# A recurrent block on one core: output product in three passes, a norm moved to ScalarE, a subtraction to GpSimd

## The reference, cut to what matters

```python
x = layernorm(x, ln0_w, ln0_b)
for l in range(4):
    h = layernorm(x, ln1_w[l], ln1_b[l]); hh = time_shift(h)
    xk, xv, xr = (h * m + hh * (1 - m) for m in (tmk[l], tmv[l], tmr[l]))
    k, v, sr = xk @ Wk[l].T, xv @ Wv[l].T, sigmoid(xr @ Wr[l].T)
    x = x + (sr * wkv(time_decay[l], time_first[l], k, v)) @ Wo[l].T
    h = layernorm(x, ln2_w[l], ln2_b[l]); hh = time_shift(h)
    xk, xr = (h * m + hh * (1 - m) for m in (cmk[l], cmr[l]))
    kf = square(relu(xk @ Wck[l].T))          # 256 -> 1024
    kv = kf @ Wcv[l].T                        # 1024 -> 256
    x = x + sigmoid(xr @ Wcr[l].T) * kv
```

## Time and profile before

| | us |
|---|---|
| median of 3 runs | 1927.9 |
| range of the runs | 1927.41 to 1932.6 |
| the profiled execution, its own time | 1932.82 |
| its span in the trace | 1931.1 |
| end of the recurrent part's last output product | about 741 |

### The profile page before, as it was taken

One profiled execution on the slowest core, in us unless ns is written; L12 is line 12 of the kernel. 1 busy time (PEld: TensorE's weight loads), 2 busy tenths in 40 slices (PEclk: granted clock), 3 DMA queues, 4 the chain that ended last, 5 costly groups with the idle time before them and its releaser, 6 DMA issues. The chain is left out here.

```text
span 1931.1 us, 26354 instructions
## 1 busy us (share of the span) xinstructions
PE 1812.3 (94%) x10124; PEld 1536.1 (80%) x10124; DVE 1233.3 (64%) x1953; ACT 841.0 (44%) x1304; POOL 2.7 (0%) x24
## 2 busy tenths in 40 slices
PE   2499999999999997999899999999999999999997
PEld 1277887777887776777689998899998899998996
DVE  6889999899998844677554454454454454454445
ACT  2565776666766543333233333333333333333333
POOL 0000000000000000000000000000000000000000
PEclk9699999999999998999789999999999999999999
DMA  3000000001001003111020000000000000001001
GB/s 109 6 22 17 12 27 34 6 28 39 1 12 49 1 1 95 42 42 36 11 76 33 34 25 10 33 33 33 33 18 14 33 33 33 33 11 60 1 1 39
DMA packets 35274, 56.54 MB, mean 29 GB/s; under 512 B 3094, under 2 KB 20476, under 8 KB 34684
## 3 DMA queue, kind: packets, MB, share of 16 engines
q1 hardware_dynamic: 35196, 55.47, 8.8%
HBM read 51.79 MB, written 3.67 MB: 29 GB/s over the span
## 5 line engine op out<-in xcount | busy, mean ns | idle before, releaser
L1489 DVE TENSOR_TENSOR hf<-sil,fbanks 128x512 f32<-128x512 f32 (+1 forms) x128 | 79.4, 620 | 332.2 <-PE fbanks L1658 273.4
L1597 ACT ACTIVATE sil<-fbanks 128x512 f32<-128x512 f32 (+1 forms) x128 | 69.6, 544 | 442.2 <-PE fbanks L1658 442.2
L1674 PE MATMUL fbank<-wl,hh 128*128 128x256 f32 x896 | 250.3, 279 | 0.0
L1674 PE MATMUL fbank<-wh,hl 128*128 128x256 f32 x896 | 250.1, 279 | 0.0
L1674 PE MATMUL fbank<-wh,hh 128*128 128x256 f32 x896 | 250.1, 279 | 0.0
L715 PE MATMUL pair<-wcv,kf 128*112 128x256 f32 x768 | 176.2, 379 | 0.0
L1489 DVE TENSOR_TENSOR hf<-sil,fbank 128x512 f32<-128x512 f32 (+1 forms) x128 | 79.5, 621 | 149.7 <-PE fbank L1658 142.7
L1674 PEld LDWEIGHTS fbank<-wl,hh 128*128 128x128 f32 x896 | 168.3, 188 | 2.2
L1674 PEld LDWEIGHTS fbank<-wh,hh 128*128 128x128 f32 x896 | 168.4, 188 | 1.8
L1674 PEld LDWEIGHTS fbank<-wh,hl 128*128 128x128 f32 x896 | 168.4, 188 | 0.0
L1496 DVE TENSOR_TENSOR hl<-hf,hh 128x512 fp32r<-128x512 f32 (+1 forms) x256 | 158.2, 618 | 0.0
(11 more groups left out here) (235 smaller groups left out, 3495.1 us busy)
## 6 DMA issues: line engine op xcount, KB each, us to landing
raw<-in_w_gate SPq DMA_DIRECT2D x16, 512.0 KB, 3.8
raw<-in_w_up SPq DMA_DIRECT2D x16, 512.0 KB, 4.7
raw<-in_w_down SPq DMA_DIRECT2D x16, 512.0 KB, 5.6
raw<-in_w_ck SPq DMA_DIRECT2D x4, 1024.0 KB, 4.8
wcv<-in_w_cv SPq DMA_DIRECT2D x4, 768.0 KB, 4.4
raw<-in_ctx_t SPq DMA_DIRECT2D x4, 750.0 KB, 6.3
ct<-in_ctx_t SPq DMA_DIRECT2D x4, 750.0 KB, 5.1
x<-in_x SPq DMA_DIRECT2D x4, 448.0 KB, 6.1
```

The source lines that it names most:

```text
L1489: dve.tensor_tensor(hf[i][:, 0:w], sil[i][:, 0:w], bank[2 * i + 1][:, 0:w], ALU.mult).then_inc(hf_ready, 1)
L1597: act.activation(sil[f % 2][:, 0:w], bank[2 * (f % 2)][:, 0:w], ACT.Silu).then_inc(sil_ready, 1)
L1674: ins = pe.matmul(bank[4 + 2 * (t % 2) + i // 2][:, (i % 2) * C:(i % 2 + 1) * C], a[t % 2][:, f, i * P:(i + 1) * P], m[h][:, DOWN + f * C: ...
```

## The change

The output product with `Wcv` takes three float32r passes for all eight blocks, and its loop runs over pairs of blocks on the outside and sequences inside: pairs 0 and 1 before `turn(1)`, pairs 2 and 3 behind it. It waits for each pair's `kfl`. The whole of `wcv` is staged and split (`wcvh`, `wcvl` of 2048 columns), and the float32 `wcv` and its DMA go. ScalarE rounds all four pairs to `kfh`. GpSimd subtracts to make `kfl`, in place of `kf`, and VectorE's `low_kf` goes. `ckl` takes the place of `mix_ck` in the same manner, and `diff` shares `dk`, for which `wkv_out` gets two waits. The second norm's `xn2` is made by ScalarE with a `shift` of its own, behind `norm_out(1)`, and the first norm's `normalise` moves ahead of `rsqrt0(2)`. On VectorE `wkv_numerator` moves ahead of `difference(1)`.

```diff
-        wcvh, wcvl = sb("wcvh", [P, SPLIT * C], F32R), sb("wcvl", [P, SPLIT * C], F32R)
-        wcv = sb("wcv", [P, (F // P - SPLIT) * C])
+        wcvh, wcvl = sb("wcvh", [P, FT * C], F32R), sb("wcvl", [P, FT * C], F32R)
...
-        shift = sb("shift", [T, G])
+        shift = {k: sb(f"shift{k}", [T, G]) for k in (1, 2)}
...
-        diff = sb("diff", [P, CB, G, T])
-        mixed = {n: sb("mix_" + n, [P, CB, G, T]) for n in ("k", "v", "r", "ck", "cr")}
+        mixed = {n: sb("mix_" + n, [P, CB, G, T]) for n in ("k", "v", "r", "cr")}
...
+        diff = dk
...
-        ckh, ckl = sb("ckh", [P, CB, G * T], F32R), sb("ckl", [P, CB, G * T], F32R)
-        kf = [sb(f"kf{i}", [P, 2, G * T]) for i in range(4)]
-        kfh, kfl = sb("kfh", [P, SPLIT, G * T], F32R), sb("kfl", [P, SPLIT, G * T], F32R)
+        ckh = sb("ckh", [P, CB, G * T], F32R)
+        with nc.sbuf_tensor("mix_ck", [P, CB, G, T], FP32) as t:
+            mixed["ck"] = t
+        ckl = sb("ckl", [P, CB, G * T], F32R)
+        with nc.sbuf_tensor("kf", [P, FT, G * T], FP32) as t:
+            kf = [t[:, 2 * j:2 * j + 2] for j in range(FT // 2)]
+        t = sb("kfl", [P, FT, G * T], F32R)
+        kfl = [t[:, 2 * j:2 * j + 2] for j in range(FT // 2)]
+        kfh = sb("kfh", [P, FT, G * T], F32R)
...
+            for m in range(STEPS):
+                for j in range(FT // 2):
+
+                    pool.wait_ge(kfh_ready, FT // 2 * m + j + 1)
+                    pool.tensor_tensor(kfl[j], kf[j], kfh[:, 2 * j:2 * j + 2], ALU.subtract).then_inc(kfl_ready, 1)
...
-                    ("cr", wcr, cr_done, 1), ("cv", wcv, cv_done, 2))
+                    ("cr", wcr, cr_done, 1))
...
-                if name == "cv":
-                    w = w[:, 0:SPLIT * C]
...
-                    t = tile if n == "cv" else tile[:].rearrange("p b c -> p (b c)")
-                    sp.dma_start(t[:, :], w[:, -t.shape[1]:]).then_inc(w_in[n], 16)
+                    sp.dma_start(tile[:].rearrange("p b c -> p (b c)"), w).then_inc(w_in[n], 16)
...
-            def set_shift(m):
-
-                dve.scalar_tensor_tensor(shift[:], mean[1], -1.0, rstd[1][:], ALU.mult, ALU.mult)\
-                    .then_inc(shift_ready, 1)
+            def set_shift(k):
+
+                dve.scalar_tensor_tensor(shift[k][:], mean[k], -1.0, rstd[k][:], ALU.mult, ALU.mult)\
+                    .then_inc(shift_ready[k], 1)
...
             def wkv_out(m):
 
                 dve.wait_ge(rec_ready, m + 1)
+                dve.wait_ge(mix1_ready, 6 * min(m + 2, STEPS))
+                if m:
+                    dve.wait_ge(mix2_ready, 4 * m)
                 after(did(dve.tensor_tensor(tokens(dk), tokens(dp), at(e1b, 1), ALU.mult)))
                 n = did(dve.scalar_tensor_tensor(tokens(dk), tokens(dk), 2.0, at(e1b, 1), ALU.subtract, ALU.mult))
                 dve.wait_ge(num_ready, m + 1)
...
-            def low_kf(m, j):
-
-                dve.wait_ge(kfh_ready, SPLIT // 2 * m + j + 1)
-                dve.tensor_tensor(kfl[:, 2 * j:2 * j + 2], kf[j][:], kfh[:, 2 * j:2 * j + 2], ALU.subtract)\
-                    .then_inc(kfl_ready, 1)
...
@@ -448,7 +448,9 @@
                     wkv_denominator(s + 1)
                 if valid(s):
                     rsqrt(2, s)
-                    normalise(2, xn[2], chunk(s), xn_ready[2])
+                    set_shift(2)
+                if valid(s + 1):
+                    wkv_numerator(s + 1)
                 if valid(s + 2):
                     n = difference(1, s + 2)
                     mix(1, s + 2, ("k", "v", "r"), ("tmk", "tmv", "tmr"), mix1_ready, n)
@@ -459,8 +461,6 @@
                     gate_channel(s - 1)
                 if valid(s):
                     mix(2, s, ("ck",), ("cmk",), mix2_ready, n)
-                if valid(s + 1):
-                    wkv_numerator(s + 1)
                 if valid(s - 1):
...
-                if valid(s):
-                    low_kf(s, 0)
                 if valid(s + 3):
                     rsqrt(1, s + 3)
-                    set_shift(s + 3)
-                if valid(s):
-                    for j in range(1, SPLIT // 2):
-                        low_kf(s, j)
+                    set_shift(1)
...
-            def normalise1(m):
-
-                act.wait_ge(shift_ready, m + 1)
+            def normalise(k, m):
+
+                act.wait_ge(shift_ready[k], m + 1)
                 xc = x[:, (m % GROUPS) * G:(m % GROUPS + 1) * G, :]
                 for i in range(G):
-                    ins = act.activation(xn[1][:, i, :], xc[:, i, :], ACT.Identity, bias=shift[:, i:i + 1],
-                                         scale=rstd[1][:, i:i + 1])
-                ins.then_inc(xn_ready[1], 1)
+                    ins = act.activation(xn[k][:, i, :], xc[:, i, :], ACT.Identity, bias=shift[k][:, i:i + 1],
+                                         scale=rstd[k][:, i:i + 1])
+                ins.then_inc(xn_ready[k], 1)
...
             def hidden(m, j):
 
                 act.wait_ge(ck_done, 4 * m + j + 1)
-                split = 2 * j < SPLIT
-                if m and split:
-
-                    act.wait_ge(kfl_ready, SPLIT // 2 * (m - 1) + j + 1)
-                if m and not split:
+                if m and j == 0:
 
                     act.wait_ge(cv_done, 2 * m)
                 t = kf[j]
-                act.activation(t[:], pair[HIDDEN[j]][:, :, 0:G * T], ACT.Relu).then_inc(relu_done, 1)
+                act.activation(t, pair[HIDDEN[j]][:, :, 0:G * T], ACT.Relu).then_inc(relu_done, 1)
                 act.wait_ge(relu_done, 4 * m + j + 1)
-                act.activation(t[:], t[:], ACT.Square).then_inc(square_done, 1)
-                if not split:
-                    return
+                act.activation(t, t, ACT.Square).then_inc(square_done, 1)
                 act.wait_ge(square_done, 4 * m + j + 1)
-                if m and j == 0:
-
-                    act.wait_ge(cv_done, 2 * m)
-                act.activation(kfh[:, 2 * j:2 * j + 2], t[:], ACT.Copy).then_inc(kfh_ready, 1)
+                act.activation(kfh[:, 2 * j:2 * j + 2], t, ACT.Copy).then_inc(kfh_ready, 1)
...
                 if valid(s + 1):
                     wkv_exp(s + 1, 2)
+                if valid(s + 2):
+                    normalise(1, s + 2)
                 if valid(s):
                     rsqrt0(2, s)
-                if valid(s + 2):
-                    normalise1(s + 2)
                 if valid(s + 1):
                     reciprocal0(s + 1)
                 if valid(s + 2):
                     norm_out(1, s + 2, pair[2], "ln1w", "ln1b")
                 if valid(s):
+                    normalise(2, s)
                     norm_out(2, s, pair[0], "ln2w", "ln2b")
                 if s < 0:
                     rsqrt0(1, s + 3)
...
-            def channel_out(m, sequences):
-                for i in sequences:
-                    n = 0
-                    for j in range(F // P):
-
-                        if i == 0 and j % 2 == 0 and j < SPLIT:
-                            pe.wait_ge(kfl_ready, SPLIT // 2 * m + j // 2 + 1)
-                        elif i == 0 and j % 2 == 0:
-                            pe.wait_ge(square_done, 4 * m + j // 2 + 1)
-                        if j < SPLIT:
-                            parts = [(a[:, j], w[:, j * C:(j + 1) * C]) for a, w in ((kfh, wcvh), (kfh, wcvl), (kfl, wcvh))]
-                        else:
-                            parts = [(kf[j // 2][:, j % 2], wcv[:, (j - SPLIT) * C:(j - SPLIT + 1) * C])]
-                        for a, w in parts:
-                            ins = pe.matmul(pair[3][0:T, i // 2, (i % 2) * C:(i % 2 + 1) * C], a[:, i * T:(i + 1) * T],
-                                            w, start=n == 0, stop=j == F // P - 1)
-                            n += 1
-                    if i % 2:
-                        ins.then_inc(cv_done, 1)
+            def channel_out(m, pairs):
+                for p in pairs:
+                    pe.wait_ge(kfl_ready, FT // 2 * m + p + 1)
+                    for i in range(G):
+                        for f in range(2):
+                            j = 2 * p + f
+                            for n, (a, w) in enumerate(((kfh[:, j], wcvh), (kfh[:, j], wcvl), (kfl[p][:, f], wcvh))):
+                                ins = pe.matmul(pair[3][0:T, i // 2, (i % 2) * C:(i % 2 + 1) * C],
+                                                a[:, i * T:(i + 1) * T], w[:, j * C:(j + 1) * C],
+                                                start=j == n == i % 2 == 0,
+                                                stop=j == FT - 1 and n == 2 and i % 2 == 1)
+                        if i % 2 and p == FT // 2 - 1:
+                            ins.then_inc(cv_done, 1)
...
                 if valid(m):
                     pe.wait_ge(wlo_ready, 2 * (m // GROUPS) + 2)
-                    pe.wait_ge(w_in["cv"], 16 * (m // GROUPS + 1))
-
                     pe.wait_ge(cth_ready, m + 1)
```

(4 more changed lines are left out.)

18 lines of the change are left out of this document (7 added, 11 removed).

## The result

The changed kernel is slower: 1966.55 us median (1964.53 to 1968.31) against 1930.25 us (1927.41 to 1932.99) for the kernel before on the same chip, a ratio of 1.0188, interval 1.0165 to 1.0210, or 36.3 us more. The forecast was 1905.5 us with a range to 1956. The profiled execution took 1967.74 us with a span of 1965.9.

What follows compares the result with a forecast made beforehand. TensorE's issue was taken to set the period; -24 us from 16 output products, +1.6 at the start and layer steps even gave -22.4 from a 1927.9 us median: 1905.5 us. Its own range was 1900 to 1915, the whole range 1900 to 1956.

Steps and rivals of the forecast that it cites:

- GpSimd's cost to VectorE: VectorE beside GpSimd's four subtractions a step: slowed by 0 to 0.7 us each, hidden in 3.2 us of room.
- Rival 1: GpSimd's reads shut out VectorE's two-input instructions, so VectorE sets a 42.5 us period; 1948 us, chance 0.38.
- It shrinks only if that sum does: Steady loop: the period is the sum of what TensorE issues, 40.52 us falling to 39.0.
- just in time: ScalarE's first norm: `xn1` at 11.6 us, less 2.4 of ended wait before `v`, meets the transposes at 9.2.
- Rival 2: ScalarE takes TensorE's place, `xn1` up to 2.4 us late; 1922 to 1932 us, chance 0.15 together with a partial hold.
- Layer steps: Steps where a layer's weights are split: TensorE waits about 1 us, as in the 41.5 us periods; counted as even.
- the output product: TensorE's product with `Wcv`: -1.5 us a step, two thirds from four changeovers becoming two; -24 us over 16 products.
- VectorE's sum without GpSimd: VectorE's work in a step: from 37.7 to 35.8 us, against 39.0 of TensorE.
- GpSimd as a wait: TensorE waiting for GpSimd's `kfl`: 0 us, since the last pair ends at 9.9 and is used at 13.0.
- the DMAs: Loading `wcv` through the staged part, 768 KB more there: 0 us.
- the start: First step, with the second norm on the serial path behind `norm_out(1)`: +1.6 us once.
- 2.4 us of cover: Second norm on ScalarE behind `norm_out(1)`: `xn2` ready at 13.4 us, TensorE wants it at 15.8.

Runs made afterwards that it cites:

- e1: The changed kernel without GpSimd's subtractions, the third pass reading `kfh` in place of `kfl` (low part of the activations left out); 1930.14 us, ratio 1.0004 to before.
- e12: e1 with VectorE's numerator behind the mixes and the gate again, plus two waits on its own mixes; 1940.58 us, ratio 1.0057 to before.
- e10: e9 with ScalarE's high part of `wcv` made ahead of the copy of `ck` in a layer step; 1940.03 us, ratio 1.0052 to before.
- b4: Kernel before with product by block pairs, four of eight blocks in three passes, first norm, numerator and high part of `wcv` early; 1926.72 us, ratio 0.9981.
- e9: e8 with the second norm on VectorE as before the change; 1958.27 us, ratio 1.0146 to before.
- e5: The changed kernel, GpSimd still subtracting, with the second norm on VectorE as before; 1987.63 us, ratio 1.0299 to before.
- e8: e1 with ScalarE making the first norm's `xn` ahead of the exponents of `eu`; 1929.14 us, ratio 0.9997 to before.
- e2: The changed kernel with GpSimd's subtraction replaced by a memset of its size, the third pass on the high part; 1929.94 us, ratio 1.0007 to before.
- e7: Kernel before plus four GpSimd subtractions of 128x896 a step on tiles of its own that no engine waits for; 2020.68 us, ratio 1.0467.
- b kernels: Four kernels, each the kernel before with parts of the change and the complete result; 1925.18, 1942.21, 1926.72 and 1928.97 us.

## Why the prediction was wrong

**The term that failed first: GpSimd's cost to VectorE.** The prediction took 0 to 0.7 us for each subtraction, "since 3.2 us of VectorE's work can slip unseen", from a term for which it had no row. It is 3.5 us a step in held instructions, of 8.6 us that GpSimd's four take alone: some of them fall beside VectorE's waits or between its instructions. Nor does 3.2 us slip unseen in each step: 1.8 us did, and in the steps with 5.6 and 7.4 us held the periods are 5.3 and 4.5 to 4.9 us longer than in e1. This was Rival 1's mechanism, in the very instructions it named. The evidence against it, "no row shows GpSimd slowing VectorE at all", was no evidence: GpSimd did nothing in that stretch before. Its length was taken as 1.8 us, measured 2.11 to 2.16 alone; the estimate from the Trainium skill, "GPSIMD Engine Reference", section 3, 1.97 us, was nearer.

**Where the rival itself was off.** It made VectorE the bound by its sum, 42.5 us in every step, without idle time. The steps are 39.9, 44.5, 41.8 and 47.7 and VectorE waits in them. Its instructions stand on the path that the norms come from, and there a held scan delays `add_wkv`, `xn2` and TensorE in turn. It also let the time start from the gain; its 1948 us lacks what the next point lost. And nothing in the prediction prices the clock: a wait of TensorE was counted at its length, and the 11.9 us of lower clock behind the long ones is a third of what the subtractions cost.

**The second failure: a smaller sum on TensorE does not make a smaller period.** "It shrinks only if that sum does" was read as "it shrinks when that sum does". Of the forecast's -22.4 us nothing came even without GpSimd (1930.14, e1). The step that failed is ScalarE's 11.6 - 2.4 = 9.2, "just in time": the wait of 2.4 us before `v` did go, but `xn1` did not come earlier by it. ScalarE's part begins with the gate, and the gate waits for TensorE's `wcr` (1.5 us a step in e1). e12 shows it from the other side: with the wait for `v` back, the regular step shown has the same wait for `xn1`. So a step started earlier by TensorE is not one started earlier by ScalarE. The meeting of the two to a tenth of a microsecond should have been read as no room. Rival 2 had this (1922 to 1932 us, TensorE waiting for `xn1`), and is what e1 is; ScalarE is not busy all the time, though, it waits at the gate.

**Layer steps.** "About 1 us, as in the 41.5 periods now" was 2.5 (42.4) and 1.8 (41.7) in e1. Four times the weights to split on ScalarE stand inside the loop, and VectorE waits up to 8.8 us for them; e10 and b4 show that in one of the two slow steps it is their place that costs (45.0 to 46.5 us became 40.9, and 43.5 to 45.2 became 39.9). The other one remains.

**Right in total, wrong in the split: the output product.** Forecast -1.5 us a step, two thirds by the changeovers; measured -1.8, all of it by the float32 blocks (24 x 0.078), none by changeovers. In the earlier trace rows the first pass behind a float32 matmul has a record of 0.47 us where the others have 0.28: it starts 0.19 us early. The twelve float32 records own 12 x 0.216 = 2.59 us and not 2.40, and 2.59 + 0.12 is the 2.71 from their start to the second pass.

**Right:** VectorE's sum without GpSimd (forecast 35.8; busy 457.6 us in 530 of e1, 35.5 a step); GpSimd as a wait, 0; the DMAs, 0; the start, +0.8 us where 1.6 was forecast. The second norm is cheaper on ScalarE than on VectorE (e9 and e5 are slower), but not free: in e8 TensorE waits 1.07 us a step for it, where the prediction had 2.4 us of cover.

**Open.** No kernel here with the whole product in three passes has a regular step below 39.8 us, although TensorE's sum is 38.7. Each edit made another result late: `xn1`, `xn2`, `mix_k`. Whether some order of ScalarE and VectorE reaches 38.7 is not settled. What brings the lower clock is open too, in the loop (single waits of up to 3.0 us in e1 left it at 1.00; one layer step of e2 took 43.2 us instead of 41.7, by 1.7 us of lower clock) and behind it.

## What to carry to other kernels

Before work goes to GpSimd, list what VectorE runs at that time: if its instructions read two SBUF tensors and GpSimd's operation reads SBUF, take the operation's whole length as the upper bound of what VectorE loses (here 3.5 and 6.3 us of 8.6 a step), and a memset at nothing. Price a new wait of TensorE above its length, since its clock may be lower behind it: look at the granted clock in the stretch after the wait. When several engines run a software pipeline, shortening the busiest one gains only down to the longest loop through the others; measure the distance from each engine's first wait to the result that the busiest one needs, and treat a sum that meets exactly as already late. Compare such kernels by the start of the last step of the loop as well as by their total, since what follows may run at another clock.

## What the runs showed of the hardware

- A GpSimd subtraction of 128x896 that reads two tiles takes 2.11 to 2.16 us alone, with one read (a copy) 1169 ns, and a memset of that size 849 ns. VectorE's instructions with two SBUF inputs that ran beside the first grew by 1.8 and 1.9 us in the timeline shown, and by 1.0 to 1.6 us on average in e7; beside the memset by nothing.
- Float32 matmuls of 256 columns start 0.216 us apart at a granted clock of 1.00, two records a block; a float32r pass starts 0.118 us behind another. Changes between the two kinds cost nothing that the step shows.
- In the changed kernel the granted clock was 0.50 for some 3.4 us in two steps of four, behind waits of TensorE of 1.2 us and then 2.7 to 4.2 us in one step, and the product with `mix_k` took 4.6 to 4.7 us from its start to the next one's instead of 3.0. In e1, steps with one wait of 3.0 us stayed at 1.00; in e2 one of them did not.
- The attention stage took 284.1 us in one profiled execution and 290.3 in another, for the same instructions and waits, at a granted clock of 0.92 and 0.90 on average. That is 0.3% of the whole time, as much as the edits of the b kernels moved.
